# Four chained attention blocks on one core: steps ordered by a table of due times, landing times of the loads in the plan, row maxima transposed as fp32r

## What is computed

```
h = group_norm(x, 32 groups, eps) * gn_w + gn_b        # statistics over 4 channels x 256 tokens
q, k, v = wq h + bq, wk h + bk, wv h + bv
blocks 0, 1, 2:  8 heads of 16 channels,  p = softmax(q.k / sqrt(16)) per head,  o = p v
block 3:         1 head of 128 channels,  p = softmax(q.k / sqrt(128)),          o = p v
x = x + wp o + bp
```

## Time and profile before

| | |
|---|---|
| median of 3 runs | 111.75 us (111.69 to 113.16) |
| the profiled execution, device time | 111.87 us |
| its span | 110.1 us |
| TensorE busy (products) | 97.5 us, 89% of the span, 932 records |
| VectorE busy | 70.8 us |
| ScalarE busy | 55.2 us |
| mean granted clock of TensorE | 0.984 of full |

### The profile page before, as it was taken

The page is one execution under the profiler, slowest core; times in us unless marked ns, Lnnn a source line. Parts: engine busy times, 40 slices in busy tenths (PEclk is TensorE's granted clock), DMA queues, the critical chain, the costliest instruction groups (busy, mean ns, idle before and its releaser), DMA issues.

```text
span 110.1 us, 2481 instructions
## 1 busy us (share of the span) xinstructions
PE 97.5 (89%) x932; PEld 75.3 (68%) x932; DVE 70.8 (64%) x188; ACT 55.2 (50%) x124; POOL 13.1 (12%) x28
## 2 busy tenths in 40 slices
PE   0299999999999689999999978999999988896991
PEld 0299987978664578779857437878886644776860
DVE  0130578998713769988871176899898027677662
ACT  4300075659596107087359840618757892025620
POOL 7000242220000013222000001052200000110000
PEclk9999999999999999999589999999999999999999
DMA  2970000000000000000000000000000000000011
GB/s 63 337 271 5 0 0 6 0 0 0 9 0 0 0 0 6 0 3 0 6 0 0 6 0 0 0 0 0 6 0 0 6 0 0 0 3 0 6 48 48
DMA packets 1739, 2.28 MB, mean 21 GB/s; under 512 B 320, under 2 KB 1216, under 8 KB 1728
## 3 DMA queue, kind: packets, MB, share of 16 engines
q1 hardware_dynamic: 1440, 1.97, 5.4%
q10 hardware_dynamic: 288, 0.16, 0.5%
HBM read 1.86 MB, written 0.26 MB: 19 GB/s over the span
## 4 chain that ended last, share of the span: by engine, by line
PE 76%; ACT 8%; DVE 6%; DMA 3%; issue 3%; ACTq 0%; DVEq 0%
PE ps L431 11%; PE ps L451 10%; PE ps L495 9%; PE ps L483 9%; ACT probs L584 6%; PE ps L406 6%; PE ps L532 5%; PE ps L469 5%; PE ps L423 4%; DMA vec<-in_vectors 3%; PE ps L438 3%; PE ps L466 3%; PE ps L517 2%; ACT o_raw L599 2%; PE ps L503 2%
## 5 line engine op out<-in xcount | busy, mean ns | idle before, releaser
L666 DVE TENSOR_REDUCE neg_max<-ps 128x2 f32<-128x512 f32 x48 | 30.5, 684 | 1.4 <-PE ps L451 1.3
L584 ACT ACTIVATE probs<-ps 128x512 f32<-128x512 f32 x48 | 25.8, 604 | 6.5 <-PE ps L483 6.4
L555 ACT ACTIVATE q_low<-ps,bias_low,const 128x256 fp32r<-128x256 f32 x12 | 6.8, 565 | 23.7 <-PE ps L431 23.6
L431 PE MATMUL ps<-hn,ws 128*128 128x256 f32 x56 | 14.5, 390 | 1.0 <-issue 0.9
L495 PE MATMUL ps<-probs,v_heads 128*32 128x256 f32 x192 | 13.4, 398 | 0.2 <-ACT probs L584 0.2
L483 PE MATMUL ps<-q_split,k_high 32*128 32x256 f32 x96 | 13.0, 330 | 0.1
L451 PE MATMUL ps<-k_high,q_split 32*128 32x256 f32 x96 | 12.2, 337 | 0.1
L431 PEld LDWEIGHTS ps<-hn,ws 128*128 128x128 f32 x56 | 9.8, 189 | 3.2 <-issue 1.7
L356 POOL TENSOR_TENSOR grp<-grp,const 128x1 f32<-128x1 f32 x8 | 4.4, 552 | 61.4 <-DVE grp L630 61.4
L483 PE MATMUL ps<-q_max,k_ext 32*128 32x256 f32 x96 | 11.1, 281 | 0.0
L451 PE MATMUL ps<-k_low,q_split 32*128 32x256 f32 x96 | 10.9, 292 | 0.0
(11 more groups left out here) (61 smaller groups left out, 147.5 us busy)
## 6 DMA issues: line engine op xcount, KB each, us to landing
w<-in_w SPq DMA_DIRECT2D x3, 384.0 KB, 5.2
xs<-in_x SPq DMA_DIRECT2D x2, 128.0 KB, 3.1
w<-in_w SPq DMA_DIRECT2D x1, 256.0 KB, 5.8
out<-xs SPq DMA_DIRECT2D x4, 64.0 KB, 1.5
const<-in_constants ACTq DMA_DIRECT2D x1, 136.0 KB, 2.9
vec<-in_vectors ACTq DMA_DIRECT2D x1, 16.0 KB, 3.7
```

Source lines behind the costliest of these rows:

```text
L431: mm(slot(*step)[:, 0:T], ws[l][:, block_of[l] + i, :], hn[b][:, :], start=True, stop=True).then_inc(done, 1)
L555: nc.scalar.activation(q_low[b][:, i, :], slot("project_q", l, b, i)[:, 0:T], ACT.Identity, bias=bias_low[:, l, i:i + 1], scale=low_rows). ...
L584: nc.scalar.activation(probs[b][:, i, :, :].rearrange("p c t -> p (c t)"), slot("scores_t", l, b, i // PACK, i % PACK)[:, :], ACT.Exp, sca ...
L666: nc.vector.tensor_reduce(neg_max[b][:, i // PER, :, QUAD * (i % PER) + MAX_ROW], slot("scores", l, b, i // PACK, i % PACK)[:, :].rearrang ...
```

## The change

1. `LEAD`, `FAVOURED` and the longest way are gone. A table `DUE` gives every step a due time (in hundredths of a microsecond; for a kind the entries run over block, image, index). `plan_order()` takes, of the steps whose needs are planned, the one that is due first, even if another could start earlier; the engine idles in the plan until then. The planned start is worked out as before.
2. `LANDED` has other values and an entry for `fold_bias` of block 0. Up to 6.5 us of the plan every TensorE step costs double, fillers too, and fillers are put into every gap there.
3. `neg_max` has the type fp32r, and the two transposing products of `turn_max` take a fp32r copy of the identity, `ident_r`, made next to `only_high` by VectorE. The plan's cost of `turn_max` goes from (.57, .8) to (.26, .55).

The diff, without the lines that only rename a semaphore or declare a tile, and without the rows of the table for steps that the text doesn't speak of:

```diff
-    "scores": ("P", .5, .68), "row_max": ("V", .6, .78), "turn_max": ("P", .57, .8), "store_max": ("A", .32, .5),
+    "scores": ("P", .5, .68), "row_max": ("V", .6, .78), "turn_max": ("P", .26, .55), "store_max": ("A", .32, .5),
...
-LANDED = {("moments", 0, 0, 0): 3.5, ("scale_w", 0, 0, 0): 4.9, ("group_means", 0, 0, 0): 4.4,
-          ("moments", 0, 1, 0): 5.6}
+LANDED = {("moments", 0, 0, 0): 3.7, ("scale_w", 0, 0, 0): 4.9, ("group_means", 0, 0, 0): 4.65,
+          ("fold_bias", 0, 0, 0): 4.9, ("moments", 0, 1, 0): 5.7}
+
+COLD_UNTIL = 6.5
 WARM = .222
 MARGIN = .3
 WINDOW, ENOUGH = 3.4, .65
 BLANK_READY = 1.
-LEAD = [17, 5, 5, -14]
-FAVOURED = {"attend": -33, "normalise": 26, "exps": -22, "turn_max": 22, "store_out": 35, "scores": -14, "scores_t": -13, "row_max": -13, "store_max": 21}
+
+
+DUE = {
+    "fold_bias": (540, 1295, 3912, 6342),
+    "add_bias": (780, 1679, 4140, 6516),
+    "moments": (370, 595, 2777, 3214, 5066, 5712, 7614, 8051),
+    "group_means": (480, 803, 2912, 3324, 5176, 5838, 7750, 8161),
...
+    "normalise": (690, 995, 3088, 3558, 5342, 6034, 7925, 8326),
+    "project_q": (760, 876, 1207, 1524, 3152, 3282, 3618, 3792, 5448, 5652, 6094, 6272, 7990, 8386),
+    "project_k": (833, 919, 1064, 1481, 3196, 3238, 3660, 3704, 5404, 5694, 6138, 6226, 8033, 8429),
+    "project_v": (962, 1250, 3510, 3746, 5868, 6180, 8076, 8706),
...
+    "turn_max": (1455, 1697, 2059, 2315, 3834, 4122, 4550, 4766, 6316, 6452, 6896, 7152),
...
+    "attend": (2085, 2225, 2576, 2728, 4410, 4576, 5056, 5220, 6922, 7062, 7414, 7565, 8751, 8661, 8976, 8915),
...
+    "turn_out": (2391, 2416, 2818, 2888, 4666, 4740, 5310, 5380, 7228, 7254, 7655, 7725),
+    "divide": (2436, 2486, 2872, 2932, 4710, 4786, 5382, 5432, 7274, 7324, 7710, 7770, 8501, 8403, 8816, 8755),
+    "scores": (1014, 1107, 1157, 1405, 1637, 1806, 1956, 2006, 3410, 3460, 3554, 3862, 4072, 4210, 4360, 4500, 5738,
+        5788, 5994, 6044, 6536, 6686, 6786, 6836, 8249, 8206, 8618, 8550),
+    "scores_t": (1567, 1756, 1856, 1906, 2175, 2341, 2441, 2491, 4022, 4160, 4260, 4310, 4690, 4792, 4876, 5006,
+        6478, 6586, 6636, 6736, 7012, 7178, 7278, 7328),
...
+    "turn_back": (2551, 2998, 4850, 5496, 7388, 7835),
...
+    "project_out": (2666, 3102, 4956, 5602, 7504, 7940, 9050, 8845, 9086, 9025),
+    "residual": (2736, 3172, 5026, 5672, 7574, 8010, 9099, 8895, 9131, 9070),
...
+def cost_at(step, start):
+
+    engine, busy, later = cost(step)
+    cold = busy if engine == "P" and start < COLD_UNTIL else 0.
+    return busy + cold, later + cold
...
-    users = {step: [] for step in needs}
-    for step, before in needs.items():
-        for other in before:
-            users[other].append(step)
-
-    rest = {}
-
-    def way(step):
-        if step not in rest:
-            rest[step] = cost(step)[2] + max([way(user) for user in users[step]], default=0.)
-        return rest[step]
+    due = {}
+    for kind, times in DUE.items():
+        due.update(zip(sorted(step for step in needs if step[0] == kind), times))
...
             start = max([starts[other] if cost(other)[0] == engine else done[other] for other in needs[step]] +
                         [free[engine], LANDED.get(step, 0.)] + [at for at, _ in open_at[:wanted]])
-            rank = (start, -way(step) - LEAD[l] * (b == 0) - FAVOURED.get(kind, 0.))
-            if best is None or rank < best[0]:
-                best = rank, step, start, [n for _, n in open_at[:wanted]]
+            if best is None or due[step] < best[0]:
+                best = due[step], step, start, [n for _, n in open_at[:wanted]]
         _, step, start, chosen = best
-        engine, busy, later = cost(step)
+        busy, later = cost_at(step, start)
         starts[step] = start
-        free[engine] = start + busy
+        free[cost(step)[0]] = start + busy
         done[step] = start + later
...
-        while t + WARM <= starts[step] - MARGIN * (warm > 0 and t > 6.):
+        while True:
+            spent = WARM * (2 if t < COLD_UNTIL else 1)
+            if t + spent > starts[step] - MARGIN * (t > COLD_UNTIL):
+                break
             active = sum(share * max(0., min(begin + busy, t) - max(begin, t - WINDOW)) for begin, busy, share in work)
             spare = [n for n in range(BANKS)
-                     if all(to <= t or begin >= t + 2 * WARM for begin, to in taken[n])]
-            if active < ENOUGH * WINDOW and spare:
+                     if all(to <= t or begin >= t + 2 * spent for begin, to in taken[n])]
+            if (t < COLD_UNTIL or active < ENOUGH * WINDOW) and spare:
                 filler = "warm", 0, 0, warm
                 starts[filler], banks_of[filler] = t, spare[:1]
-                work.append((t, WARM, 1.))
+                work.append((t, spent, 1.))
                 warm += 1
-            t += WARM
-        work.append((starts[step], cost(step)[1], ROWS_USED.get(step[0], 1.) if step[1] < MULTI else 1.))
+            t += spent
+        work.append((starts[step], cost_at(step, starts[step])[0], ROWS_USED.get(step[0], 1.) if step[1] < MULTI else 1.))
     return sorted(starts, key=starts.get), banks_of
...
+        neg_max = [sb(f"neg_max{b}", [C, SETS, NCH, C], F32R) for b in range(B)]
...
                 elif kind == "turn_max":
                     if l == b == i == 0:
-                        pe.wait_ge(only_high_ready, 1)
+                        pe.wait_ge(selectors_ready, 2)
                     bank_free(step)
                     dst = slot(*step)
                     mm(dst[:, 0:T], only_high[:, :], q_split[b][:, i, :], start=True, stop=False)
                     pe.wait_ge(max_done, nth("row_max", l, b, PER * (i + 1) - 1))
                     for qc in range(NCH):
-                        last = mm(dst[:, qc * CHUNK:(qc + 1) * CHUNK], neg_max[b][:, i, qc, :], ident,
+                        last = mm(dst[:, qc * CHUNK:(qc + 1) * CHUNK], neg_max[b][:, i, qc, :], ident_r[:, :],
                                   start=False, stop=(qc == NCH - 1))
                     last.then_inc(max_turned, 1)
...
                 elif kind == "add_bias":
                     if l == 0:
                         dve.wait_ge(const_in, 16)
-                        ts(only_high[:, :], ident, high_rows, None, ALU.mult).then_inc(only_high_ready, 1)
+                        ts(only_high[:, :], ident, high_rows, None, ALU.mult).then_inc(selectors_ready, 1)
+                        ts(ident_r[:, :], ident, 1.0, None, ALU.mult).then_inc(selectors_ready, 1)
                     dve.wait_ge(bias_folded, nth("fold_bias", l, b))
                     link(tt(bias[:, l, :], slot("fold_bias", l, 0)[:, 0:NBIAS], vec[:, l, BQ:BV + 1], ALU.add))
```

More of the change, by code:

```diff
@@ L71 @@
 BLANK_READY = 1.
-LEAD = [17, 5, 5, -14]
-FAVOURED = {"attend": -33, "normalise": 26, "exps": -22, "turn_max": 22, "store_out": 35, "scores": -14, "scores_t": -13, "row_max": -13, "store_max": 21}
+DUE = {
+    "scale_w": (490, 1319, 3936, 7707),
+    "fold_bias": (540, 1295, 3912, 6342),
+    "add_bias": (780, 1679, 4140, 6516),
+    "moments": (370, 595, 2777, 3214, 5066, 5712, 7614, 8051),
+    "group_means": (480, 803, 2912, 3324, 5176, 5838, 7750, 8161),
+    "variance": (570, 863, 2982, 3432, 5236, 5908, 7820, 8221),
+    "rsqrt": (610, 903, 3022, 3472, 5276, 5948, 7860, 8261),
+    "normalise": (690, 995, 3088, 3558, 5342, 6034, 7925, 8326),
+    "project_q": (760, 876, 1207, 1524, 3152, 3282, 3618, 3792, 5448, 5652, 6094, 6272, 7990, 8386),
+    "project_k": (833, 919, 1064, 1481, 3196, 3238, 3660, 3704, 5404, 5694, 6138, 6226, 8033, 8429),
+    "project_v": (962, 1250, 3510, 3746, 5868, 6180, 8076, 8706),
+    "store_v": (1169, 1409, 3574, 3812, 5932, 6246, 8389, 8802),
+    "mask_q": (840, 941, 1272, 1589, 3218, 3346, 3682, 3856, 5512, 5716, 6402, 6450),
+    "round_k": (898, 988, 1129, 1546, 3264, 3304, 3730, 3770, 5470, 5764, 6202, 6290),
+    "split_q": (905, 1035, 1398, 1820, 3308, 3456, 3878, 4100, 5624, 5868, 6476, 6556),
+    "split_k": (954, 1076, 1237, 1719, 3350, 3390, 3838, 4240, 5582, 5934, 6434, 6598),
+    "extend_k": (1014, 1136, 1297, 1779, 3528, 3598, 3898, 4300, 5642, 6004, 6494, 6658),
+    "turn_max": (1455, 1697, 2059, 2315, 3834, 4122, 4550, 4766, 6316, 6452, 6896, 7152),
+    "store_max": (1510, 1752, 2122, 2374, 3904, 4188, 4604, 4820, 6370, 6508, 6952, 7212),
+    "attend": (2085, 2225, 2576, 2728, 4410, 4576, 5056, 5220, 6922, 7062, 7414, 7565, 8751, 8661, 8976, 8915),
+    "store_out": (2195, 2342, 2707, 2838, 4526, 4686, 5199, 5330, 7032, 7180, 7544, 7675),
+    "turn_out": (2391, 2416, 2818, 2888, 4666, 4740, 5310, 5380, 7228, 7254, 7655, 7725),
[4 more added lines that the diff above has]
+        6478, 6586, 6636, 6736, 7012, 7178, 7278, 7328),
+    "row_max": (1117, 1177, 1278, 1338, 1439, 1499, 1559, 1619, 1760, 1861, 1921, 1981, 2041, 2101, 2161, 2221, 3498,
+        3598, 3658, 3718, 3778, 3920, 3980, 4040, 4180, 4282, 4342, 4402, 4462, 4522, 4582, 4642, 5808, 5974, 6074,
```

(23 more changed lines are left out.)

## The result

Twenty executions of the changed kernel had a median of 114.88 us (112.84 to 125.23), twenty of the kernel before 111.77 us. The ratio is 1.0145, with an interval of 1.0117 to 1.0172. The profiled execution took 112.84 us, with a span of 111.0. The prediction was 101.4 us, its range 97.5 to 105.5, and it gave a change of less than 2%, which this is, 0.03, by another mechanism than the one that came.

What follows compares the result with a forecast made beforehand. TensorE bounds the kernel, busy 97.5 of 110.1 us, with a chain of waits at the start. 111.87 - 5.9 (start) - 2.6 (maxima) + 1.0 - 1.0 - 0.8 - 1.2 (order) = 101.4 us, range 97.5 to 105.5.

Steps and rivals of the forecast that it cites:

- rival (c): Clock: two more falls, with `fold_bias` before packs in layers 1 and 2, and a slow start: 105.6 us, chance 0.12.
- The start: Up to the first projection: new landing times put `fold_bias` behind `group_means` and moments ahead of `add_bias`, -5.9 us.
- The maxima: Twelve `turn_max` steps, four fp32 records becoming two fp32r: 0.22 us each, -2.6 us (0 to -3.8).
- the smaller gain by the rule about row groups: In `turn_max`, if loads overlap products only where row groups differ: 0.12 us a step, 1.4 in all.
- The order: Due times across the layers: lone packs +1.0, layer ends -1.0 and -0.8, smaller waits -1.2 us.
- +1.0: Packs of `scores` and `scores_t` losing their neighbour on the other row half, 13 lone instead of 8: net +1.0 us.
- -1.0: End of layer 0: last `attend` of image 1 moves beside the residual and moments, where TensorE idled: -1.0 us.
- - 0.8: End of layer 1: `turn_back` and `project_out` of image 1 fill the place of fillers and a wait: -0.8 us.
- -1.2: Smaller waits, 5.7 us spread over the layers and last block, a fifth taken as gone: estimated -1.2 us.

Runs made afterwards that it cites:

- the control: The kernel before with only the one-column products of `fold_bias` given 128 columns: 110.78 us, ratio 0.989.
- the best kernel: The changed kernel with `fold_bias` on 128 columns, `group_means` products repeated to 120 columns and 8 more fillers: 103.17 us, ratio 0.9235.
- the greedy order: The kernel before's order, run with new landing times, cold-start fillers and 128-column `fold_bias`: median 106.04 us with fp32 maxima, 107.7 with fp32r.
- the widened kernel: The changed kernel with the five one-column products of each `fold_bias` given 128 columns: 104.38 us median, ratio 0.917.

## Why the prediction was wrong

**The clock is the step that failed.** The sum of terms priced TensorE's steps at the clock of the kernel before, and put what the change itself does to the clock at nothing; rival (c) had the mechanism, and even the place ("right before runs of packs in layers 1 and 2"), but was mis-sized. It took a fall to last as long as the one seen, 3.4 us, and cost 1.15 us. That price nearly holds for such a fall (0.94 us between the traces of the control). But a fall has no fixed length. In the changed kernel it lasted 23.9 us and cost 19.58 - 11.25 = 8.3 us in the part measured above, 0.7 ahead of it (from `turn_max` to the `attend` 49.09 - 45.09 = 4.0 us, against 50.45 - 47.18 = 3.27) and 0.55 behind it (from the first projections of layer 2 to the next ones 71.58 - 68.67 = 2.91 us, against 64.06 - 61.70 = 2.36). The fall at the start cost 1.6 us: from the first projection to pack 1 of `scores` 12.62 - 6.94 = 5.68 us, where the best kernel needs 10.95 - 6.87 = 4.08. Together 11.2 us, 10% of the execution: 112.84 - 11.2 = 101.6, beside the 102.0 that was measured at full clock with the same order and a wide `fold_bias`. That this is near the 101.4 predicted is partly luck: with the clock up the order gave less than its term and the maxima up to 0.5 us more, as said below, and the old kernel's fall, 0.94 us that the prediction left in, is gone too. The Trainium skill (TensorE: Matmul & The Clock Gate, Part 1) says that the clock follows how busy TensorE has been. This trace doesn't agree, if busy is what the profile counts: it shows 23.9 us at the lower level with TensorE busy throughout. The same part puts the cost of the slow beginning, not of later falls, under 1% of a typical span. The run with fp32 maxima in the new order doesn't agree there: it reached the first `project_k` of image 1 at 13.72 us, the same kernel with the wide `fold_bias` at 10.49, and the 3.2 us between them are 3% of the span.

**The start**: -5.9 predicted. 5.2 measured between executions recorded at full clock, and the first projection is 6.6 us earlier in the trace. Right.

**The maxima**: -2.6 predicted. The step went from 0.76 to 0.49 us, 12 x 0.27 = 3.2 in the trace; end to end 2.0 us in the greedy order (105.6 to 103.57) and 1.7 to 3.1 in the table's (105.1 to 103.44 and 102.0, both at full clock). Right in size. The two transposing products take 45.58 - 45.31 = 0.27 us together where four records took 0.54, so the smaller gain by the rule about row groups (0.12 us a step) didn't come true. What the prediction didn't ask is what else the removed work did: it helped to keep the clock up, as the four executions with the fp32r maxima alone show (0.858 to 0.969).

**The order**: -2.0 net predicted (+1.0 - 1.0 - 0.8, and -1.2 estimated as a fifth of 5.7 us, which is 1.1, without a row that says where). Measured with fp32 maxima: 0 to 0.5 us. With the fp32r ones only single executions stand beside each other at full clock, 103.57 us in the greedy order, 103.44 and 102.0 in the table's. This is the second step that failed. Of the 1.5 us at the end of layer 0 some 0.9 is a real gain, close to the -1.0. The price of a lone pack held, 0.67 us (14.00 to 14.67 in the trace of the table's order), but the count was too low. In the orders that the two kernels plan, 10 packs have no neighbour on the other half before and 20 after; the prediction counted 8 and 13, as it left out neighbours on the same half, most of them in layers 0 and 1, which don't overlap either (two of them from 16.29 to 17.43, 0.57 each, where overlapping ones take 0.35). At these prices, less its two packs that didn't overlap before, the term is an estimated 2.1 us (3 x 0.32 + 5 x 0.22) and not 1.0. The -1.2 was seen nowhere.

**The chances**: 0.94 for faster rested on the start, which no rival could take back except the clock; (c) should have been given an open end, since the trace before couldn't show what ends a fall.

**Open**: what in the work makes the clock fall, and what holds it down once it has fallen. That lone packs and the short maxima do it is argued from what lies in the stretch, not shown: with one-column products, executions fell in the new order with fp32 maxima (118.97 us), in the old one with fp32r maxima (122.29) and also in the old order with the old maxima and the new start (115.62). The new start and the fp32r maxima are thus each enough by themselves in some executions; the new order was run only together with the new start. The kernel before, which has none of the three, stayed at 0.967 or above in the executions beside them. Why the same kernel falls in one execution and not in the next wasn't tried.

## What to carry to other kernels

Work that a tuned kernel does beside its result can be what keeps TensorE's clock up: before taking work off a dense TensorE, look for the stretches where its products are narrow (that few rows matter too was not shown here), and price a fall by the work that would follow it, not by the length of the last one. Give narrow products their full columns where the record takes almost as long anyway. Judge each edit at equal clocks: put the granted clock of every execution beside its time, and read the spacing of the records at the start, where the recorded clock can be wrong, since a median over mixed clocks called the new start worthless (112.45) when it was worth 5 us. And when an order moves work past the mark that a stretch is measured by, measure between marks with the same work behind them.

## What was not expected of the hardware

- An fp32 product of one column costs almost as much as one of 128: the ten records of `fold_bias` take 43.94 - 42.74 = 1.20 us with one column (profile after) and 46.03 - 44.72 = 1.31 us with 128 (the widened kernel), 0.12 and 0.13 us apart.
- Products without a gap don't by themselves bring the clock up: 23.9 us of them ran at 1.2 GHz in the changed kernel, and at one start some 11 us with hardly a gap (1.03 to about 12.3 us in the new order with fp32 maxima).
- The granted clock reads 1.00 before its first recorded change, while fillers, `fold_bias` and projections run at half the rate.
- An fp32r product of 128 columns by 128: two of them in 0.33 us, the whole `turn_max` in 0.49 us.
